# Soft mixture, layer 3: the slots' reciprocal lengths by ScalarE and VectorE, and GpSimd's fills behind the first beta

## What is computed

```python
xn = _layernorm(x, ln_gamma, ln_beta)
x_unit = _l2norm(xn, axis=-1)
mu_unit = _l2norm(mu, axis=0)            # mu: 128 features x (16 experts * 16 slots)
logits = einsum('bnd,des->bnes', x_unit * scale, mu_unit)
dispatch = softmax(logits, axis=1)
combine = softmax(logits.reshape(B, N, E * S), axis=-1).reshape(B, N, E, S)
slot_in = einsum('bnd,bnes->besd', xn, dispatch)
h = gelu(einsum('besd,edh->besh', slot_in, w1) + b1, approximate=False)
slot_out = einsum('besh,ehd->besd', h, w2) + b2
out = einsum('besd,bnes->bnd', slot_out, combine)
```

## Time and profile before

| | us |
|---|---|
| median of three executions | 3386.78 |
| lowest, highest | 3386.07, 3394.66 |
| the profiled execution | 3393.24 |
| its span, first to last instruction | 3391.0 |

### The profile page before, as it was taken

The page is one execution under the profiler, slowest core; times in us unless marked ns, Lnnn a source line. Parts: engine busy times, 40 slices in busy tenths (PEclk is TensorE's granted clock), DMA queues, the critical chain, the costliest instruction groups (busy, mean ns, idle before and its releaser), DMA issues. The chain is left out here.

```text
span 3391.0 us, 57590 instructions
## 1 busy us (share of the span) xinstructions
PE 3122.1 (92%) x20342; PEld 2432.0 (72%) x20342; DVE 2531.4 (75%) x5358; ACT 1701.6 (50%) x3925; POOL 893.4 (26%) x707
## 2 busy tenths in 40 slices
PE   5999998978878799999389999999999999999998
PEld 4767674545454577878267888888888888888887
DVE  4878775867767654555386888888888888888888
ACT  2545543221212244343165666666666666666666
POOL 2101000010100200000552344444444444444443
PEclk9999998989899889899799999999999999999999
DMA  2001101000000000000300000000100000000000
GB/s 52 2 4 51 50 1 47 1 1 0 1 0 1 1 1 1 1 1 1 76 1 1 21 21 9 22 15 20 22 21 21 21 9 21 15 20 21 21 1 26
DMA packets 43552, 53.05 MB, mean 16 GB/s; under 512 B 8645, under 2 KB 27272, under 8 KB 43272
## 3 DMA queue, kind: packets, MB, share of 16 engines
q1 hardware_dynamic: 39298, 47.02, 5.6%
q10 hardware_dynamic: 3974, 2.37, 0.3%
HBM read 38.63 MB, written 10.75 MB: 15 GB/s over the span
## 5 line engine op out<-in xcount | busy, mean ns | idle before, releaser
L75 PE MATMUL banks<-scratch 128*128 128x128 f32 (+3 forms) x3648 | 715.6, 325 | 11.5 <-ACT scratch L2670 8.9
L75 PE MATMUL banks<-nT,w 128*128 128x512 f32 x1184 | 588.3, 616 | 52.4 <-DVE hidden L1562 35.5
L75 PEld LDWEIGHTS banks<-scratch 128*128 128x128 f32 x3648 | 482.9, 192 | 77.0 <-issue 60.2
L75 PEld LDWEIGHTS banks<-scratch,tb 128*128 128x128 f32 x2560 | 356.6, 191 | 102.0 <-issue 61.6
L75 PE MATMUL banks<-scratch,tb 128*128 128x128 f32 x2560 | 368.5, 275 | 0.0
L3116 POOL TENSOR_TENSOR scratch<-scratch,aT 128x1024 f32<-128x1024 f32 x128 | 359.2, 2806 | 4.5 <-DVE aT L2938 4.5
L75 PEld LDWEIGHTS banks<-nT,w 128*128 128x128 f32 x1184 | 205.6, 196 | 213.2 <-issue 146.1
L83 DVE SCALAR_TENSOR_TENSOR scratch<-scratch,tb 128x512 f32<-128x512 f32 (+3 forms) x512 | 340.4, 706 | 8.4
L3108 POOL TENSOR_TENSOR scratch<-backwards,nn 128x512 f32<-128x512 f32 x128 | 133.1, 1040 | 735.9 <-ACT nn L3028 735.9
L83 DVE SCALAR_TENSOR_TENSOR scratch<-tb,nn,banks 128x512 f32<-128x512 f32 (+3 forms) x512 | 267.7, 544 | 76.3 <-PE banks L75 72.1
L2938 DVE TENSOR_TENSOR aT<-banks,turn 64x1024 f32<-64x1024 f32 x256 | 312.8, 1222 | 5.7
(11 more groups left out here) (391 smaller groups left out, 5418.0 us busy)
## 6 DMA issues: line engine op xcount, KB each, us to landing
tb<-head_rows SPq DMA_DIRECT2D x32, 512.0 KB, 7.0
turn<-head_turns SPq DMA_DIRECT2D x64, 128.0 KB, 2.7
head_turns<-loads SPq DMA_DIRECT2D x16, 256.0 KB, 2.8
head_turns<-rotation SPq DMA_DIRECT2D x16, 256.0 KB, 2.9
xs<-in_x SPq DMA_DIRECT2D x8, 256.0 KB
w<-in_L_Wqk SPq DMA_DIRECT2D x16, 128.0 KB, 2.1
out<-xs SPq DMA_DIRECT2D x8, 256.0 KB, 2.3
w<-in_L_w1T SPq DMA_DIRECT2D x1, 1280.0 KB, 9.3
```

The lines of the kernel that those rows point to most:

```text
L75: return self.T.matmul(out, lhsT, rhs, start=start, stop=stop, skip_group_check=True)
```

## The change

The reciprocal lengths of the slots are no longer a power on GpSimd. ScalarE takes the square root of the clamped squared lengths, in place, inside `square` of block 0 (after its wait for beta, before the square), and VectorE takes the reciprocal, in place, inside `unit_rows` of block 0, just ahead of the multiplication of mu; `step` makes VectorE wait for its own result. The semaphore `m3_length`, which GpSimd counted up, is now counted up by ScalarE. The fills and the select of `own` and `backwards` stand behind beta of block 0 instead of ahead of the slots.

```diff
--- before.py
+++ after.py
@@ -2548,6 +2548,7 @@
             k.m3_filled_by(V, 1, "units", b - 2)
             if b == 0:
                 V.wait_ge(k.m3_length.sem, 1)
+                k.step(V.reciprocal(k.mu_scratch[:, 1, :], k.mu_scratch[:, 1, :]))
                 V.tensor_tensor(k.mu3[:, :], k.mu3[:, :], k.mu_scratch[:, 1, :], ALU.mult).then_inc(*k.m3_mu.up())
             for t in range(TPB):
                 m = k.ts(k.moe[:, j * TPB + t, :], k.lanes_m[j]["xn"][:, t, :], k.m3_rows[j]["ru"][:, t:t + 1])
@@ -2633,6 +2634,9 @@
             j = b % 2
             A.wait_ge(k.m3_xb.sem, b + 1)
             k.after(A, k.m3_ss, b - 1)
+            if b == 0:
+                k.m3_emptied_of(A, 7, "directions")
+                A.activation(k.mu_scratch[:, 1, :], k.mu_scratch[:, 1, :], ACT.Sqrt).then_inc(*k.m3_length.up())
             A.activation(k.normed[:, j * TPB:(j + 1) * TPB, :], k.lanes_m[j]["xn"], ACT.Square).then_inc(*k.m3_sq.up())
 
         def open_copy(b):
@@ -2717,7 +2721,7 @@
         k, G = self, self.G
 
         def done():
-            for count in (k.pool, k.m3_r, k.m3_rr, k.m3_xb, k.m3_ru, k.m3_hm, k.m3_length):
+            for count in (k.pool, k.m3_r, k.m3_rr, k.m3_xb, k.m3_ru, k.m3_hm):
                 k.after(G, count, count.n)
 
         def small(inst, count=None):
@@ -2751,15 +2755,18 @@
             done()
             G.wait_ge(k.m3_xg.sem, b + 1)
             small(G.tensor_tensor(x, x, k.bet[:, :].unsqueeze(1).broadcast_to([P, TPB, D]), ALU.add), k.m3_xb)
+            if b == 0:
+                done()
+                k.fill(k.own[:, :, :], 0.0)
+                for e in range(4):
+                    for c in range(2):
+                        k.fill(k.own[32 * e:32 * e + 32, c, 64 * c + 16 * e:64 * c + 16 * e + 16], 1.0)
+                k.fill(k.backwards[:, :], 0.0)
+                k.keep_where(k.backwards[:, :], ALU.not_equal, 1.0, 1 - P, [[1, P]], 1)
 
         def unit_power(b):
             r = k.m3_rows[b % 2]
             done()
-            if b == 0:
-                m = k.mu_scratch[:, 1, :]
-                k.m3_emptied_of(G, 7, "directions")
-                small(G.tensor_tensor(m, m, k.minus_half[:, 0:1].broadcast_to([P, 256]), ALU.pow), k.m3_length)
-                G.wait_ge(k.m3_length.sem, 1)
             G.wait_ge(k.m3_ss.sem, b + 1)
             k.after(G, k.m3_xu, b - 1)
             small(k.ts(r["ru"], r["ss"], 1e-24, None, ALU.max, eng=G))
@@ -2774,12 +2781,6 @@
             k.m3_emptied_of(G, 6, "hidden", b)
             small(G.tensor_tensor(g, g, k.own[:, :, :].unsqueeze(1).broadcast_to([P, 2, 2, P]), ALU.mult), k.m3_hm)
 
-        k.fill(k.backwards[:, :], 0.0)
-        k.keep_where(k.backwards[:, :], ALU.not_equal, 1.0, 1 - P, [[1, P]], 1)
-        k.fill(k.own[:, :, :], 0.0)
-        for e in range(4):
-            for c in range(2):
-                k.fill(k.own[32 * e:32 * e + 32, c, 64 * c + 16 * e:64 * c + 16 * e + 16], 1.0)
         for s in k.m3_slots():
             if 0 <= s < SEQS:
                 first_power(s)
```

## The result

The changed kernel takes 3351.38 us, the median of four executions (3347.59 to 3353.12), against 3388.99 for the kernel before (3386.07 to 3394.66, four). The ratio is 0.9885, with a 95% interval from 0.9868 to 0.9903: 37.6 us less. The prediction was 3348.7 within 3343 to 3357, and 38.07 us less. The profiled execution took 3347.59 us, its span is 3345.5.

A forecast was written before the change was run, and what follows sets the result against it. GpSimd's 128x256 power was taken to bound the mixture's opening. Power and gap 41.21, plus 1.04 at the head, less fills 2.40 and reciprocal 1.78, give 38.07 us; 3386.78 less that is 3348.7 us, range 3343 to 3357.

The forecast's parts named there:

- What bounds the kernel: Opening of the soft mixture: GpSimd's 128x256 power, 41.13 us, holds block 0's row lengths and every engine behind them.
- the third rival: GpSimd's 41.13 us row is something else holding it; only additions remain, 3.1 us more, 3389.9 us; 3%.
- The fills: On GpSimd, moved behind beta: first small operation through beta 1.04 us earlier, but 2.40 us still ahead of the row lengths.
- The loads: Latest load gamma waits for is covered by 0.6 us; otherwise waiting could take up to the whole 1.04 us gain.
- The root: ScalarE's root, 0.38 us, and its table loads cost nothing, covered by 2.1 us before GpSimd wants the sum.
- the first rival: ScalarE's two table loads are exposed, 2.56 us, giving 3351.3 us; 5%.
- The reciprocal: VectorE's 128x256 reciprocal, behind the wait for block 0's row lengths, all on the path: 1744 ns, 1.78 us with visibility.
- The sum: VectorE's product of mu starts at 1659.91 instead of 1697.98, 38.07 us earlier.
- The same slow start: TensorE still starts at its lower clock after the shorter idle; up to 1.84 us less or some microseconds more.
- the second rival: TensorE's clock rises later, so block 0's transposes and slot sums run at half speed: 4 to 5 us, 3353; 8%.
- The median: Whole kernel time: median of three before, 3386.78, less 38.07, gives 3348.7 us.
- The fourth rival: The heads' 128 units fall into a longer period; at 0.4 us a unit, 3400 us; 2%.

The follow-up runs named there:

- power: Two kernels: the kernel before with GpSimd's power over 128 of 256 columns, 3375.78 us, or over 32 of 128 partitions, 3398.12 us.
- fills alone: The kernel before with only the fills and select moved behind beta of block 0, the power staying on GpSimd; 3400.08 us.
- root alone: The changed kernel with the fills left in front, so only root and reciprocal replace the power; 3349.04 us, ratio 0.9886.

## Why the prediction was right

- **What bounds the kernel.** Right. The power's row was its own and all on the path: it scales with the columns, not with the rows, and starts later if it is put later (power, fills alone). With that the third rival is out.
- **The fills.** The 1.04 us at the head came as counted at the first operation (2.40 to 1.36), at scale and at gamma (1641.45 is 5.12 from the start, 6.16 before). At beta 0.76 was left: from gamma's end to beta it is 0.45 us instead of 0.17. The traces with the fills behind a beta all show the longer gap, those with the fills in front (root alone, and both smaller powers) the old one; why is open. Behind beta the fills took 2.39 us for the 2.40 counted. That they are still on the path is shown by the fills put later, 2.25 us.
- **The loads.** The cover was given as 0.6 us. It was 0.48: the load of scale, issued at 1637.67, landed 3.3 us later, at 1640.97, and gamma began at 1641.45, released by GpSimd.
- **The root.** Counted at nothing, and nothing it was: the sum was ready at 1646.00, the row lengths started at 1648.43. The cover was given as 2.1 us; it was 2.3 (1648.43 - 1646.00 less 0.17). The root took 0.42 us for the 0.38 taken. That nothing of it was exposed holds for the fills in their new place alone: with the fills in front it cost 0.34 us, with the fills later 0.1. The load back had its idle stretch, so the first rival is out. By the page ScalarE: Activation LUTs of the Trainium skill (What ACT_TABLE_LOAD costs) a drain of some 1.4 us comes on top of each load; here the root starts at 1644.34, 0.06 us after the load's end.
- **The reciprocal.** 1744 ns by the two neighbouring shapes, 1.75 us measured, all of it on the path: 1.73 us came back when it went ahead of the wait.
- **The sum.** 38.07 at the product; 53.50 - 15.69 = 37.81 measured. The missing 0.26 is the late beta (0.28), the other terms being off by 0.03 at most.
- **From the product to the end.** "The same slow start" was right: it was there before and after, and it costs 2.25 us, shown by keeping TensorE busy. The range given for the clock, 1.84 us less to some more, holds the two executions of the changed kernel, 1.25 us more and 0.03 less than before. What the sum did not have is a second fall of the clock at the slot sums of block 0: 1.66 us in the profiled execution, of which an earlier rise gave 0.39 back in the first logits, and none in the other. It is the second rival in small, in some executions only, and not by that rival's mechanism: the rise came 4.7 us from the first transposes, sooner than the 7.7 of before, and then the clock fell again.
- **The median.** The prediction took 3386.78 for the kernel before; four executions gave 3388.99, so 2.2 of the 2.7 us by which the time lies above the forecast are that term, the median of three. The 28 further executions of that kernel lie between 3380.16 and 3396.91, with a median of 3390.4. So 37.6 against 38.07 agrees closer than the measurement can tell (its interval is some 6 us to either side), and that closeness is luck; what bears the prediction out is 37.81 at the product, read within the traces. The 8.15 us by which mu's load comes earlier in the trace of after would have made the gain 46 if spans alone were compared (3391.0 - 3345.5 = 45.5).
- **The fourth rival** did not show: the heads to the end took between 1571.5 and 1572.9 us in all fourteen traces.

## What to carry to other kernels

Price a power on GpSimd by the elements of a partition before putting it on a path that others wait for: over 256 of them it held the core for 41 us, while VectorE's reciprocal and ScalarE's root did it in 2.2, with two table loads of 1.28 us in idle stretches. When a step is moved, ask whether its new place is still ahead of the operation that all wait for, and whether a wait that it does not need stands in front of it: the fills and the reciprocal cost 2.25 and 1.73 us for that alone. Compare two traces from a landmark at the start of the changed stretch, since the part ahead of it may differ by more than the edit.

## What the runs showed of the hardware

- GpSimd's power takes the same 41.12 us over 32 partitions as over 128, and 20.73 for half the columns.
- TensorE's clock fell in an idle of some 6 us behind 5.69 us of work (20 matmuls), and stayed up where the idle was 0.16 us. The first filling gained nothing, the second 2.25 us. In another version 13 matmuls left an idle of 3.36 us, and the clock fell in the first logits; 25 left 0.54 us, the first logits ran at the higher level, and a fall at the slot sums stayed.
- The same layers ahead of the mixture end anywhere within 18 us in fourteen traces (1633.30 to 1651.51 for mu's load). TensorE's granted clock differs there between executions, 0.97 in the earliest of these traces and 0.92 in the latest from 200 to 400 us; whether it is the whole cause was not tried.
